# Graph layers on one core: the first two gathers of each layer moved into the block ahead of it

## The chip, the cores and the metric

The kernel runs on 1 core of one Trainium2 chip, in one launch. The metric is the device time of an execution in microseconds (us); the number compared is the median of several runs. A profile is one execution of its own, with its own time.

## What is computed

A graph with 50000 nodes of 64 features and 100000 directed edges (25000 drawn ones in both directions and 50000 self loops, sorted by target) goes through two NGCF layers, then a residual sum and a layer norm:

```python
def _ngcf_conv(x, W1, W2, src, dst, n_nodes):
    deg_out = clip(segment_sum(ones, src), 1.0)
    deg_in = clip(segment_sum(ones, dst), 1.0)
    norm = rsqrt(deg_out[src] * deg_in[dst])
    msg = (x[src] @ W1 + x[src] * x[dst] @ W2) * norm[:, None]
    agg = segment_sum(msg, dst)
    return x @ W1 + agg
h = relu(_ngcf_conv(x, W1_1, W2_1, ...))
h = _ngcf_conv(h, W1_2, W2_2, ...)
out = layernorm(x + h)
```

## The kernel before, in words

Nodes lie in 392 tiles of 128; tile t, lane p is row p * 392 + t of a table in HBM. The program is a chain of blocks, and in a block each engine has its own list of instructions, with waits on semaphores between them.

- **prepare** (the block of lines 84 to 437) reads the edge lists, sorts the edges into 398 chunks of 128 edges of neighbouring targets, counts degrees, makes the norms, and writes `k.row_i` (L422), the table row of each edge's source, and `table0`: x beside its norm, 65 floats a row. The table goes out in six stores on SP's queue (L183), each as soon as its norms are made (L417). SP waits at L184 to L186 until all stores have landed. `spread` (two tiles, written at L392, read by the matmuls at L268) is a work tile of this block alone. GpSimd's last work here is iota at about 22 us; after it the engine has nothing to do in this block.
- **layer** (called twice, its block opens at L516 and following) goes in 51 batches of 8 chunks (the last two have 4 and 2). GpSimd (L652 to L657) issues one indirect DMA a chunk, which gathers 128 rows of the table into `rows`, a ring of 4 batches. Before batch b from the fifth on it waits until batch b - 4 is used up: in layer 0 by VectorE's first step on it (`rows_scaled`, L892), in layer 1 by TensorE's sums (`summed`, L676). Within the list there is no other order. VectorE makes the selection matrices (`select`, L885), in layer 0 also cuts the rows into three bf16 parts (`cut`, L892, L895, L898); TensorE adds up each tile with three matmuls a pair of chunk and tile (`add_up`, L676); then come the node's own row, norms, the product with the weights (L705, L762, L698), relu or layer norm, and the stores: in layer 0 into `table1`, 96 floats a row (L632), in layer 1 into the output (L635). SP waits at L648 until the stores have landed.

Between two blocks stands a barrier over all five engines that the library writes at a block's end. In the compiled program it reads so: TensorE, VectorE, ScalarE and SP each drain, add one to a first semaphore and wait for a second; GpSimd drains, waits until the first has four, and then releases the others with the second. So GpSimd leads: nobody enters the next block before its drain is through. `rows` and the semaphores `gathered` belong to the layer (L527, L559), so no gather can be issued before this barrier.

The only waits between the landing of the last store and the first gather are that barrier's. The same holds ahead of layer 1.

Of the kernel before, what the change touches and what calls it, by code (L numbers as in the profile page):

```python
# [7 lines left out]
P = 128  # L8
N_NODES, D, N_EDGES = 50000, 64, 100000
EPS = 1e-5  # L10
F32 = mybir.dt.float32
I32 = mybir.dt.int32
F16 = mybir.dt.float16
BF16 = mybir.dt.bfloat16
ALU = mybir.AluOpType
# [3 lines left out]
TILES = 392  # L19
# [11 lines left out]
LOW = 1024  # L31


def band(c):

    return range(max(0, (P * c - REACH) // CAP + 1), min(TILES - 1, (P * c + P - 1) // CAP) + 1)
# [18 lines left out]
FRAME_TILE = [4 * p for p in FRAME_P0]  # L55
FRAME_SHIFT = [round((FRAME_TILE[k] + FRAME_TILE[k + 1]) / 2 * (CAP - P) / P) for k in range(FRAMES)]
SPAN = 64
PIECES = [(k, b, 4) for k in range(7) for b in (0, 4)] + [(7, 0, 8), (8, 0, 8)]
LAST_PIECE = [max(i for i, p in enumerate(PIECES) if p[0] == k) for k in range(FRAMES)]

# [19 lines left out]
def prepare(nc, x, src, dst, tables, keepers):  # L80
# [3 lines left out]
    with ExitStack() as ctx:  # L84
        def sb(name, shape, dt=F32):
            return ctx.enter_context(nc.sbuf_tensor("a_" + name, shape, dt))

        def sem(name):
            return ctx.enter_context(nc.semaphore("a_" + name))
# [5 lines left out]
        def scratch(width=RUN, dt=F32):  # L95
# [17 lines left out]
        value_t = [sb(f"value_t{a}", [P, RAWS], F16) for a in range(4)]  # L113
        hot = [sb(f"hot{j}", [P, P, 4 * FRAME_PS[0]], F16) for j in range(3)]
        near_s, near_n = sb("near_s", [P, WIN, EB * FRAME_PS[0]], F16), sb("near_n", [P, WIN, EB * FRAME_PS[0]], F16)
        spread = [sb(f"spread{j}", [P, 4, WIN, EB * FRAME_PS[0]], F16) for j in range(2)]
        node_grid = sb("node_grid", [P, TILES + SPAN])
        root, square = sb("root", [P, TILES]), sb("square", [P, TILES])
        row_f = sb("row_f", [P, CHUNKS])
# [9 lines left out]
        hots_made, spread_made, piece_placed, added = sem("hots_made"), sem("spread_made"), sem("piece_placed"), sem("added")  # L129
        number16_made, differed, deg_made, root_made, norm_step, norm_made = (sem(n) for n in (  # L130
            "number16_made", "differed", "deg_made", "root_made", "norm_step", "norm_made"))
        tail_made, table_out = sem("tail_made"), sem("table_out")
        x_in = [sem(f"x_in{i}") for i in range(len(X_LOADS) + 1)]
        block = ctx.enter_context(nc.Block())

# [52 lines left out]
        @block.gpsimd  # L188
        def _(pool):
            G = nc.gpsimd  # L190
            free = dict(allow_small_or_imprecise_dtypes=True)


            G.iota(num, pattern=[[1, RUN]], base=0, channel_multiplier=RUN, **free).then_inc(built, 1)
            pool.wait_ge(built, 1)
            G.affine_select(out=num, in_=num, compare_op=ALU.is_ge, fill=float(NO_EDGE), base=N_EDGES - 1,
                            pattern=[[-1, RUN]], channel_multiplier=-RUN).then_inc(num_made, 1)
            G.memset(k.ident[:, :], 0.0).then_inc(built, 1)
            pool.wait_ge(built, 2)
            G.affine_select(out=k.ident[:, :], in_=k.ident[:, :], compare_op=ALU.not_equal, fill=1.0,  # L200
                            base=0, pattern=[[-1, P]], channel_multiplier=1).then_inc(built, 1)
            G.memset(step16[:, :], 0.0).then_inc(built, 1)
            G.memset(wrap16[:, :], 0.0).then_inc(built, 1)
            pool.wait_ge(built, 3)
            G.tensor_copy(ident16[:, :], k.ident[:, :]).then_inc(consts, 1)
            G.iota(lanes[:, :, :], pattern=[[1, P], [0, FRAME_PS[0]]], base=0, channel_multiplier=0, **free).then_inc(consts, 1)
            pool.wait_ge(dst_in, 48)
            G.tensor_scalar(shifted_i, d_i[:, 0:RUN], float(-SHIFT * P), None, ALU.add).then_inc(shifted_made, 1)
            G.iota(home[:, :], pattern=[[1, EB // 2], [0, 2], [4, EP]], base=0, channel_multiplier=0, **free).then_inc(consts, 1)
            pool.wait_ge(kept_made, 1)  # L210
            pool.wait_ge(float_made, 1)
            G.tensor_tensor(number, kb, node_f, ALU.subtract).then_inc(built, 1)
            pool.wait_ge(built, 6)
            G.tensor_scalar(number_h, number, float(LOW), 1.0 / 64, ALU.add, ALU.mult).then_inc(number_made, 1)
            G.iota(win_s[:, :, :], pattern=[[1, WIN + max(FRAME_SHIFT)], [0, FRAME_PS[0]]], base=-BACK, channel_multiplier=0, **free).then_inc(consts, 1)
            G.iota(win_n[:, :, :], pattern=[[1, WIN], [0, FRAME_PS[0]]], base=-BACK - SHIFT, channel_multiplier=0, **free).then_inc(consts, 1)
            G.affine_select(out=step16[:, :], in_=step16[:, :], compare_op=ALU.not_equal, fill=64.0,
                            base=0, pattern=[[-1, P]], channel_multiplier=1).then_inc(built, 1)
            pool.wait_ge(built, 7)
            G.affine_select(out=step16[:, :], in_=step16[:, :], compare_op=ALU.not_equal, fill=-64.0,  # L220
                            base=1, pattern=[[-1, P]], channel_multiplier=1).then_inc(consts, 1)
            G.affine_select(out=wrap16[:, :], in_=wrap16[:, :], compare_op=ALU.not_equal, fill=-64.0,
                            base=1 - P, pattern=[[P, P]], channel_multiplier=1).then_inc(consts, 1)
            for i in range(0, LOW + 4 * P, LOW):
                n = min(LOW, LOW + 4 * P - i)
                last = G.iota(k.place[:, i:i + n], pattern=[[1, n]], base=1, channel_multiplier=0, **free)
            last.then_inc(consts, 1)

        @block.tensor
        def _(pe):  # L230
# [92 lines left out]
        def _(dve):  # L323
# [95 lines left out]
            def row_numbers(a, b):  # L419
                step(V.scalar_tensor_tensor(row_f[:, a:b], k.grid[:, 1, BACK + a:BACK + b], float(TILES), k.grid[:, 0, BACK + a:BACK + b], ALU.mult, ALU.add))  # L420
                step(V.tensor_scalar(row_f[:, a:b], row_f[:, a:b], float(-TILES), 0.0, ALU.add, ALU.max))
                V.tensor_single_scalar(k.row_i[:, a:b], row_f[:, a:b], float(P * TILES), op=ALU.min)  # L422


            V.tensor_reduce(k.extreme[0:EP, 1:2], step_up, AX.X, ALU.min).then_inc(checked, 1)
# [47 lines left out]
GROUP = [(t, t + 8) for t in range(0, TILES - 8, 8)] + [(TILES - 8, TILES - 4), (TILES - 4, TILES)]  # L473
GROUPS = len(GROUP)
GN = 8
RING = 4
BANKS = 3

COUNT_AT = [{b: b for b in range(0, 44, 2)}, {b: b for b in range(1, 45, 2)}]
# [33 lines left out]
def layer(nc, l, x, out, tables, flag, keepers):  # L513

    k = keepers
    with ExitStack() as ctx:  # L516
        def sb(name, shape, dt=F32):
            return ctx.enter_context(nc.sbuf_tensor(f"c{l}_" + name, shape, dt))

        def sem(name):  # L520
            return ctx.enter_context(nc.semaphore(f"c{l}_" + name))
# [1 line left out]
        def ps(name, shape):  # L523
            return ctx.enter_context(nc.psum_tensor(f"c{l}_" + name, shape, F32))

        row = (ROW, THREE)[l]
        rows = sb("rows", [P, RING, 8, row])  # L527
        sel = sb("sel", [P, 2, 8, 4 * P], BF16)
        hot_l, hot_t = sb("hot_l", [P, 8, P], F16), sb("hot_t", [P, 8, TILES], F16)
        own = sb("own", [P, 2, GN, D])  # L530
# [8 lines left out]
        else:  # L539
# [16 lines left out]
        tail_out = sem("tail_out")  # L556
        own_end_made, end_in, end_total, settled, w_made, last_made = (sem(n) for n in (
            "own_end_made", "end_in", "end_total", "settled", "w_made", "last_made"))
        gathered = [sem(f"gathered{j}") for j in range(RING)]  # L559
        stored, res_in = [sem(f"stored{j}") for j in range(4)], [sem(f"res_in{j}") for j in range(3)]  # L560
        block = ctx.enter_context(nc.Block())
        x_full = x[0:FULL_TILES * P, :].rearrange("(t p) d -> p t d", p=P)
# [87 lines left out]
        @block.gpsimd  # L650
        def _(pool):
            for b in range(BATCHES):  # L652
                done(pool, (rows_scaled, summed)[l], b - RING + 1)
                for i in range(BATCH[b]):
                    c = FIRST[b] + i
                    nc.gpsimd.indirect_dma_start(out=rows[:, b % RING, i], out_offset=None, in_=tables[l],  # L656
                                                 in_offset=bass.IndirectOffsetOnAxis(ap=k.row_i[:, c:c + 1], axis=0)).then_inc(gathered[b % RING], 16)  # L657

        @block.tensor
        def _(pe):  # L660
# [766 lines left out]
class Kept:  # L1427


    def __init__(k, keep, ctx, weights):  # L1430
        k.weights = weights
        k.ident, k.ones, k.eps = (keep(n, [P, w], F32, ctx) for n, w in (("ident", P), ("ones", 1), ("eps", 1)))
        k.place = keep("place", [P, LOW + 4 * P], F16, ctx)
        k.wcat = keep("wcat", [2 * D, 2, D], F32, ctx)

        k.grid = keep("grid", [P, 3, CHUNKS + 10], F32, ctx)
        k.row_i = keep("row_i", [P, CHUNKS], I32, ctx)

        k.number16 = keep("number16", [P, TILES + 1], F16, ctx)
        k.deg = keep("deg", [P, TILES], F32, ctx)  # L1440
        k.extreme, k.tally = keep("extreme", [P, 2], F32, ctx), keep("tally", [P, 4], F32, ctx)
        k.xh = keep("xh", [P, TILES, ROW], F32, ctx)

# [4 lines left out]
def build(nc, x, src, dst, weights, out, dram):  # L1448
    tables = [dram["table0"], dram["table1"]]
    with ExitStack() as last:  # L1450
        def keep(name, shape, dt=F32, stack=last):
            return stack.enter_context(nc.sbuf_tensor("k_" + name, shape, dt))
        flag = keep("flag", [1, 1], I32)
        with ExitStack() as ctx:
            k = Kept(keep, ctx, weights)
            prepare(nc, x, src, dst, tables, k)
            k.p_count = ctx.enter_context(nc.psum_tensor("k_p_count", [P, 512], F32))
            for l in range(2):
                layer(nc, l, x, out, tables, flag, k)

        def if_needed(eng):
            return eng.If(eng.value_load(flag[0:1, 0:1]) > 0)
        general_path(nc, x, src, dst, weights, out, dram, if_needed)
# [18 lines left out]
```

## Time and profile before

| what | value |
|---|---|
| three runs | 1763.13, 1771.59, 1775.89 us, median 1771.59 |
| profiled execution, its own time | 1784.15 us |
| its span, first to last instruction | 1782.5 us |
| mean granted TensorE clock in it | 0.725 of full speed |

The span is 1.65 us short of the execution's own time, and that is 12.6 us (0.7%) above the median of the three runs, which themselves lie within 0.7%. Times in the rows are microseconds from the span's start. A row's last part in brackets is the idle time of the engine just before it and what ended it; SPq, PEq and POOLq are the queues (sequencers) of these engines.

### The profile page before, as it was taken

The numbers are of one execution on the slowest core, as the hardware profiler recorded it, in microseconds if no ns is written. First come the engines' busy times: TensorE is split into PE (matmuls) and PEld (weight loads), VectorE is DVE, ScalarE is ACT, GpSimd is POOL, SyncE is SP. The second block draws the span as 40 slices with busy tenths as digits, with TensorE's granted clock in tenths as the row PEclk, the third lists the DMA queues.
The fourth block names the chain that finished last, engine by engine and source line by source line (L and its number), as shares of the span: only waits on it lengthen the run. The fifth ranks groups of instructions, "written<-read, shape, count | busy, mean of one in ns | idle before, by whom it ended". The sixth has DMA issues, their size and how long they took to land. (4 is left out here: it accounts for less than half of the span.)

```text
span 1782.5 us, 33246 instructions
## 1 busy us (share of the span) xinstructions
PE 998.9 (56%) x12938; PEld 862.4 (48%) x12938; DVE 1001.7 (56%) x2595; ACT 741.0 (42%) x2743; POOL 789.1 (44%) x819
## 2 busy tenths in 40 slices
PE   2641455565456456644665526666666666666666
PEld 2530344454355345544555525555555555555556
DVE  9982354555355445543565714665656656656556
ACT  2000144454354434543455602444444445444445
POOL 4007454344434443454343165555554555545540
PEclk9999866676676666766667856767767777767767
DMA  7951011111111111111111211222322222222222
GB/s 146 244 214 27 15 37 35 31 42 44 37 31 43 44 34 31 42 45 35 31 43 41 88 35 36 59 62 63 78 63 62 63 63 63 63 62 63 63 62 51
DMA packets 148569, 106.57 MB, mean 60 GB/s; under 512 B 115832, under 2 KB 128568, under 8 KB 147900
## 3 DMA queue, kind: packets, MB, share of 16 engines
q1 hardware_dynamic: 122728, 71.17, 14.6%
q0 software_dynamic: 25472, 32.86, 10.0%
q8 instruction: 102, 1.67, 0.4%
q10 hardware_dynamic: 212, 0.42, 0.1%
q14 instruction: 55, 0.45, 0.1%
HBM read 59.27 MB, written 45.11 MB: 59 GB/s over the span
## 5 line engine op out<-in xcount | busy, mean ns | idle before, releaser
L656 POOL DMA_INDIRECT c_rows<-table,k_row_i x796 | 768.2, 965 | 952.5 <-DVE c_yr L892 342.3
L676 PE MATMUL c_sum<-c_rows,c_sel 128*128 128x64 bf16 x4665 | 267.6, 224 | 274.6 <-issue 253.8
L762 ACT ACTIVATE c_uvt<-c_turn 128x512 f32<-128x512 f32 x196 | 106.6, 595 | 705.6 <-PE c_turn L705 703.0
L676 PEld LDWEIGHTS c_sum<-c_rows,c_sel 128*128 128x128 bf16 x4665 | 233.3, 119 | 307.6 <-issue 304.2
L930 DVE TENSOR_TENSOR c_sum<-c_sum,c_own 128x512 f32<-128x512 f32 x94 | 65.6, 698 | 507.5 <-PE c_sum L676 495.2
L676 PE MATMUL c_sum<-c_rest,c_sel 128*128 128x64 bf16 x1555 | 223.0, 219 | 134.3 <-issue 134.3
L676 PE MATMUL c_sum<-c_yr,c_sel 128*128 128x64 bf16 x1555 | 223.4, 219 | 131.3 <-issue 106.8
L676 PE MATMUL c_sum<-c_lo,c_sel 128*128 128x64 bf16 x1555 | 223.8, 219 | 109.4 <-issue 109.2
L885 DVE TENSOR_SCALAR c_sel<-k_place,k_grid 128x512 bf16<-128x512 f16 (+2 forms) x796 | 228.9, 358 | 86.0 <-PE c_sum L676 86.0
L676 PEld LDWEIGHTS c_sum<-c_yr,c_sel 128*128 128x128 bf16 x1555 | 177.3, 117 | 155.8 <-issue 155.6
L676 PEld LDWEIGHTS c_sum<-c_rest,c_sel 128*128 128x128 bf16 x1555 | 173.9, 115 | 143.4 <-issue 143.0
L698 PE MATMUL c_out<-k_wcat,c_uvt 128*128 128x64 f32 x1504 | 206.0, 295 | 59.9 <-ACT c_uvt L762 46.0
L698 PEld LDWEIGHTS c_out<-k_wcat,c_uvt 128*128 128x128 f32 x1504 | 193.6, 208 | 87.1 <-ACT c_uvt L762 65.9
L676 PEld LDWEIGHTS c_sum<-c_lo,c_sel 128*128 128x128 bf16 x1555 | 173.9, 115 | 120.0 <-issue 119.6
L754 ACT ACTIVATE c_sum<-c_sum,k_xh 128x64 f32<-128x64 f32 x752 | 161.6, 317 | 156.9 <-DVE c_sum L930 156.9
L741 ACT ACTIVATE c_own<-k_xh 128x64 f32<-128x64 f32 x752 | 193.4, 398 | 9.9 <-PEq L84 7.7
L705 PE MATMUL c_turn<-k_ident,c_uv 128*128 128x128 f32 x784 | 147.1, 350 | 0.7 <-DVE c_uv L968 0.7
L918 DVE TENSOR_SCALAR c_hot_t<-k_place,k_grid 128x392 f16<-128x392 f16 x398 | 131.6, 331 | 0.0
L705 PEld LDWEIGHTS c_turn<-k_ident,c_uv 128*128 128x128 f32 x784 | 122.5, 187 | 1.0 <-DVE c_uv L968 1.0
L967 DVE TENSOR_TENSOR c_uv<-c_sum,k_xh 128x512 f32<-128x512 f32 (+1 forms) x100 | 67.7, 677 | 85.9 <-ACT c_sum L754 49.3
L917 DVE TENSOR_SCALAR c_hot_l<-k_place,k_grid 128x128 f16<-128x128 f16 x398 | 99.0, 249 | 0.0
L807 ACT ACTIVATE c_y<-c_z,c_rstd 128x64 f32<-128x64 f32 x368 | 93.7, 371 | 0.3 <-DVE c_rstd L1010 0.3
(162 smaller groups left out, 1053.2 us busy)
## 6 DMA issues: line engine op xcount, KB each, us to landing
table<-c_y SPq DMA_DIRECT2D x48, 384.0 KB
c_rows<-table,k_row_i POOLq DMA_INDIRECT x796
out<-c_y SPq DMA_DIRECT2D x48, 256.0 KB
c_res<-in_x SPq DMA_DIRECT2D x46, 256.0 KB
table<-k_xh SPq DMA_DIRECT2D x2, 3640.0 KB, 10.9
table<-k_xh SPq DMA_DIRECT2D x1, 3542.5 KB, 12.1
table<-k_xh SPq DMA_DIRECT2D x1, 1040.0 KB, 7.0
c_res_end<-in_x SPq DMA_DIRECT2D x1, 704.0 KB, 6.3
```

The costliest lines, as they stand in the source:

```text
L656: nc.gpsimd.indirect_dma_start(out=rows[:, b % RING, i], out_offset=None, in_=tables[l], in_offset=bass.IndirectOffsetOnAxis(ap=k.row_i[:, ...
L676: last = nc.tensor.matmul(p_sum[g % BANKS][:, t - GROUP[g][0], :], sel[:, b % 2, i, n * P:(n + 1) * P], part[:, i], start=first and q == 0 ...
L698: last = nc.tensor.matmul(out_bank(g)[:, n, :], uvt[:, g % 2, n, :], weights, start=True, stop=True)
L705: last = nc.tensor.transpose(turn_bank(g, n)[:, n % 4, :], uv[:, g % 2, n].rearrange("p a d -> p (a d)"), k.ident[:, :])
L741: last = A(own[:, g % 2, t - a, :], k.xh[:, t, 0:D], ACT.Copy, scale=k.xh[:, t, D:ROW])
L754: last = A(p_sum[g % BANKS][:, t - a, :], p_sum[g % BANKS][:, t - a, :], ACT.Copy, scale=k.xh[:, t, D:ROW])
L762: last = A(uvt[:, g % 2, h:h + 4, :], turn_bank(g, h)[:, :, :], ACT.Copy)
L807: last = A(y[:, g % 4, n, :], z[:, g % 4, n, :], ACT.Copy, scale=rstd[:, g % 4, n:n + 1])
L885: last = V.tensor_scalar(sel[:, b % 2, i, 0:w], k.place[:, a:a + w], k.grid[:, 2, BACK + c:BACK + c + 1], None, ALU.is_equal)
L917: V.tensor_scalar(hot_l[:, m], k.place[:, 0:P], k.grid[:, 1, slot], None, ALU.is_equal)
L918: last = V.tensor_scalar(hot_t[:, m], k.place[:, 0:TILES], k.grid[:, 0, slot], None, ALU.is_equal)
L967: V.tensor_tensor(uv[:, j, 0:w, 0, :], bank[:, 0:w], h, ALU.add)
```

## The change

`rows` becomes a part of a tile `k.ring` that is kept over all blocks, and so do the semaphores `gathered`. In prepare the two `spread` tiles lie in the same memory. GpSimd's list in prepare gets three waits at its end (row numbers made, the zero rows and the six stores landed) and then chunks 0 and 1 of layer 0's batch 0. Its list in layer 0 gets four waits at its end (all stores of `table1` landed) and then chunks 0 and 1 of layer 1. Both layers start at chunk 2.

```diff
+RING = 4
+BEGUN = 2
+def ring_of(k, l):
+    row = (ROW, THREE)[l]
+    return k.ring[:, 0:RING * 8 * row].rearrange("p (r c d) -> p r c d", r=RING, c=8)
+
+def gather(nc, k, l, tables, b, i):
+    c = FIRST[b] + i
+    return nc.gpsimd.indirect_dma_start(out=ring_of(k, l)[:, b % RING, i], out_offset=None, in_=tables[l],
+                                        in_offset=bass.IndirectOffsetOnAxis(ap=k.row_i[:, c:c + 1], axis=0)).then_inc(k.gathered[l][b % RING], 16)
...
+SPREAD = 4 * WIN * EB * FRAME_PS[0]
...
-        spread = [sb(f"spread{j}", [P, 4, WIN, EB * FRAME_PS[0]], F16) for j in range(2)]
+        spread = [k.ring[:, j * SPREAD // 2:(j + 1) * SPREAD // 2].bitcast(F16).rearrange("p (a w r) -> p a w r", a=4, w=WIN) for j in range(2)]
...
@@ prepare, gpsimd, at the end
             last.then_inc(consts, 1)
+            pool.wait_ge(rows_made, 2)
+            pool.wait_ge(zero_out, 32)
+            pool.wait_ge(table_out, 16 * len(NORM_TILES))
+            for i in range(BEGUN):
+                gather(nc, k, 0, tables, 0, i)
...
@@ prepare, vector, row_numbers
-                V.tensor_single_scalar(k.row_i[:, a:b], row_f[:, a:b], float(P * TILES), op=ALU.min)
+                V.tensor_single_scalar(k.row_i[:, a:b], row_f[:, a:b], float(P * TILES), op=ALU.min).then_inc(rows_made, 1)
...
@@ layer
-        row = (ROW, THREE)[l]
-        rows = sb("rows", [P, RING, 8, row])
+        rows, gathered = ring_of(k, l), k.gathered[l]
...
-        gathered = [sem(f"gathered{j}") for j in range(RING)]
...
@@ layer, gpsimd
                 done(pool, (rows_scaled, summed)[l], b - RING + 1)
-                for i in range(BATCH[b]):
-                    c = FIRST[b] + i
-                    nc.gpsimd.indirect_dma_start(out=rows[:, b % RING, i], out_offset=None, in_=tables[l],
-                                                 in_offset=bass.IndirectOffsetOnAxis(ap=k.row_i[:, c:c + 1], axis=0)).then_inc(gathered[b % RING], 16)
+                for i in range(BEGUN if b == 0 else 0, BATCH[b]):
+                    gather(nc, k, l, tables, b, i)
+            if l == 0:
+                for j in range(4):
+                    pool.wait_ge(stored[j], 16 * len(range(j, GROUPS, 4)))
+                for i in range(BEGUN):
+                    gather(nc, k, 1, tables, 0, i)
...
@@ Kept
+        k.ring = keep("ring", [P, max(RING * 8 * THREE, 2 * SPREAD // 2)], F32, ctx)
+        k.gathered = [[ctx.enter_context(nc.semaphore(f"k_gathered{l}_{j}")) for j in range(RING)] for l in range(2)]
```

## Rows read from the trace of the kernel before

**Rows 1.** The page, part 1: busy us, share of the span, instructions

```profile
PE 998.9 (56%) x12938; PEld 862.4 (48%) x12938; DVE 1001.7 (56%) x2595; ACT 741.0 (42%) x2743; POOL 789.1 (44%) x819
```

**Rows 2.** The page, part 5: groups; busy, mean ns | idle before, releaser

```profile
L656 POOL DMA_INDIRECT c_rows<-table,k_row_i x796 | 768.2, 965 | 952.5 <-DVE c_yr L892 342.3
L676 PE MATMUL c_sum<-c_rows,c_sel 128*128 128x64 bf16 x4665 | 267.6, 224 | 274.6 <-issue 253.8
...
L676 PE MATMUL c_sum<-c_rest,c_sel 128*128 128x64 bf16 x1555 | 223.0, 219 | 134.3 <-issue 134.3
```

**Rows 3.** Timeline of layer 0's first 20 us: start, us, engine, line

```profile
123.36 0.67 SPq L183 DMA_DIRECT2D table<-k_xh  x1
129.34 2.02 ACT L741 ACTIVATE c_own<-k_xh 128x64 f32<-128x64 f32 x8 [7.73 <-PEq L84]
129.37 0.15 DVE L1014 TENSOR_SCALAR c_checks<-k_extreme 128x1 f32<-128x1 f32 x1 [6.04 <-PEq L84]
130.10 1.17 POOL L656 DMA_INDIRECT c_rows<-table,k_row_i  x1 [107.78 <-POOLq L84]
...
131.58 0.94 POOL L656 DMA_INDIRECT c_rows<-table,k_row_i  x1 [0.30 <-issue]
132.83 0.94 POOL L656 DMA_INDIRECT c_rows<-table,k_row_i  x1 [0.30 <-issue]
```

**Rows 4.** Waits of SP's queue: us in total, times, longest us

```profile
SPq L186 <- DMA table<-k_xh: 4.8, 1, 4.8
...
SPq L648 <- DMA table<-c_y: 1.5, 1, 1.5
```

**Rows 5.** Timeline where layer 1 begins

```profile
1011.36 2.30 SPq L632 DMA_DIRECT2D table<-c_y  x3
...
1015.69 2.02 ACT L741 ACTIVATE c_own<-k_xh 128x64 f32<-128x64 f32 x8 [2.15 <-PEq L516]
...
1016.31 0.99 POOL L656 DMA_INDIRECT c_rows<-table,k_row_i  x1 [41.73 <-POOLq L516]
1017.60 0.94 POOL L656 DMA_INDIRECT c_rows<-table,k_row_i  x1 [0.30 <-issue]
1018.84 0.94 POOL L656 DMA_INDIRECT c_rows<-table,k_row_i  x1 [0.30 <-issue]
```

**Rows 6.** Chain of waits from layer 1's start: start, us, what

```profile
1015.55 0.02 POOLq L516
1015.56 0.74 issue
1016.31 0.99 POOL c_rows L656
...
1025.08 2.24 DMA c_rows<-table,k_row_i
...
1027.69 2.50 PE c_sum L676 x44
...
1045.53 2.59 issue
1048.11 0.21 PE c_sum L676
```

**Rows 7.** Timeline of a wait for VectorE's cut in mid layer 0

```profile
751.94 1.27 POOL L656 DMA_INDIRECT c_rows<-table,k_row_i  x1 [16.26 <-DVE c_yr L892]
...
751.00 0.68 DVE L892 TENSOR_TENSOR c_yr<-c_rows 128x512 f32<-128x512 f32 x1
```

**Rows 8.** Timeline of VectorE at both layers' starts

```profile
131.55 2.34 DVE L885 TENSOR_SCALAR c_sel<-k_place,k_grid 128x128 bf16<-128x128 f16 x8
141.61 0.69 DVE L892 TENSOR_TENSOR c_yr<-c_rows 128x512 f32<-128x512 f32 x1 [7.72 <-DMA c_rows<-table,k_row_i]
...
198.18 1.93 DVE L885 TENSOR_SCALAR c_sel<-k_place,k_grid 128x512 bf16<-128x512 f16 x7 [44.21 <-PE c_sum L676]
...
1015.93 4.49 DVE L885 TENSOR_SCALAR c_sel<-k_place,k_grid 128x128 bf16<-128x128 f16 x16
1062.25 2.54 DVE L885 TENSOR_SCALAR c_sel<-k_place,k_grid 128x512 bf16<-128x512 f16 x8 [41.83 <-PE c_sum L676]
```

**Rows 9.** Busy us by stretch; PE, PEld, DVE, ACT, POOL, clock, DMA share, GB/s

```profile
130.00:190.00 60.00, 6.25 (x60) 4.16 (x61) 13.72 (x43) 1.36 (x6) 45.57 (x48) 1.00 0.17 27
190.00:200.00 10.00, 3.86 (x22) 1.99 (x22) 1.82 (x7) 0.00 (x0) 0.25 (x1) 1.00 0.03 4
1016.00:1056.00 40.00, 5.55 (x60) 3.91 (x60) 4.42 (x17) 1.71 (x8) 30.24 (x32) 0.50 0.28 58
```

More of the change, by code:

```diff
@@ L131, in prepare @@
             "number16_made", "differed", "deg_made", "root_made", "norm_step", "norm_made"))
-        tail_made, table_out = sem("tail_made"), sem("table_out")
+        tail_made, table_out, rows_made = sem("tail_made"), sem("table_out"), sem("rows_made")
         x_in = [sem(f"x_in{i}") for i in range(len(X_LOADS) + 1)]
@@ L475 @@
 GN = 8
-RING = 4
 BANKS = 3
@@ L1427, with __init__ @@
 class Kept:
-    def __init__(k, keep, ctx, weights):
+    def __init__(k, nc, keep, ctx, weights):
         k.weights = weights
@@ L1454, in build @@
         with ExitStack() as ctx:
-            k = Kept(keep, ctx, weights)
+            k = Kept(nc, keep, ctx, weights)
             prepare(nc, x, src, dst, tables, k)
```

## The prediction

> **What bounds the kernel now.** I read the page first. No engine is busy for much over half of the span [rows 1], so the time is made of waits. The widest groups say which: GpSimd idles for 952.5 us before its gathers, mostly for VectorE's cuts, and TensorE's sums idle for 274.6 us on "issue", time in which nothing that the profile shows was awaited [rows 2]. So in the middle of a layer GpSimd has slack, and a gather is worth nothing there. It can be worth something only where the ring is empty, at the two starts, so I went to the timeline and the chain of waits there.
>
> Layer 0's start: the last table store is issued at 123.36 and SP's queue is through with it at 124.03 [rows 3]; SP then waits 4.8 us for its landing [rows 4], so it lands at about 128.83. ScalarE and VectorE begin in the new block at 129.34 and 129.37, GpSimd's first gather at 130.10 [rows 3]: 1.27 us after the landing. Layer 1's start: the last store leaves SP's queue at 1011.36 + 2.30 = 1013.66 [rows 5], SP waits 1.5 us [rows 4], landing at 1015.16. GpSimd releases the barrier at 1015.55 [rows 6], ScalarE begins at 1015.69, the first gather at 1016.31 [rows 5]: 1.15 us after the landing. Both starts lie on the path that sets the end: VectorE waits 7.72 us for layer 0's first batch [rows 8], and the chain of waits goes through layer 1's first eight gathers and the landing of the eighth to TensorE's first sum at 1027.69 [rows 6].
>
> What follows the first sum matters too. TensorE does some 50 of batch 0's 75 matmuls at full pace and then creeps, with pauses of up to 2.59 us for one matmul of 0.21 us [rows 6]: 60 matmuls in 60 us in layer 0 and 60 in 40 us in layer 1, while GpSimd issues 48 and 32 gathers one behind the other [rows 9]. Batch 0's sum is done at 198.18 and 1062.25, where VectorE's select goes on [rows 8], some 8 and 6 us after GpSimd's run of gathers has ended. I take it that the creep ends when GpSimd's run does, so that what GpSimd gains at a start is gained one for one.
>
> **The change part by part.** First the gathers. A gather occupies GpSimd for 0.94 us, the next starts 0.30 us later, and a first one takes up to 1.17 us [rows 3] or 1.27 us [rows 7]. Two of them, from the first's start to the third's, are 132.83 - 130.10 = 2.73 us in layer 0 [rows 3] and 1018.84 - 1016.31 = 2.53 us in layer 1 [rows 5]. Were both wholly hidden, 5.3 us would be gained: that is the most. But nothing new hides them. They can't start before the table has landed, and that is the very event that opens the barrier. All there is to overlap is the barrier's own passage, 1.27 and 1.15 us. And GpSimd leads that barrier: its drain stands behind the two gathers, so the release waits for them, and the other four engines are held.
>
> Layer 0, step by step. From a wait that opens to a gather's start, GpSimd needs 751.94 - (751.00 + 0.68) = 0.26 us [rows 7]. So the first gather starts at 128.83 + 0.26 = 129.09. The second follows as before after 131.58 - 130.10 = 1.48 us, at 130.57, and ends at 131.51. Then drain, barrier, branch. From GpSimd's release to its first gather it was 0.76 us (0.02 and 0.74) in layer 1 [rows 6]. The drain and the check of the four signals, all there by then, no row shows. They cost no less than nothing and no more than the 0.39 us from landing to release in layer 1 (1015.16 to 1015.55), in which SP's own drain lies too; I take 0.1, since SP's steps fall away. The third gather thus starts at 131.51 + 0.1 + 0.76 = 132.37, before at 132.83: 0.46 us gained, between 0.17 and 0.56.
>
> Layer 1: first gather at 1015.16 + 0.26 = 1015.42, the second 1.29 us later at 1016.71, its end at 1017.65, third at 1018.51, before at 1018.84: 0.33 us gained, between 0.04 and 0.43. The four waits on `stored` stand behind a GpSimd that idled for 41.73 us [rows 5], and three of the four are open long before; they cost nothing.
>
> Second, the others are released later. ScalarE begins 0.14 us after the release in layer 1 [rows 5, 6], so the release was at about 129.2 in layer 0; now it is at 131.6, and in layer 1 at 1017.75 instead of 1015.55: later by 2.4 and 2.2 us. Queued behind are ScalarE's own rows, VectorE's checks and selects and SP's fetches. VectorE's select ends at 133.89 and the engine then waits till 141.61 [rows 8]: 7.7 us of cover for 2.4. In layer 1 its 16 selects end at 1020.42, and TensorE wants them only with the rows at 1027.69. So this costs nothing; without the cover it would be 4.6 us in all. Third, the signal on the row numbers and GpSimd's waits in prepare: the engine was idle for 107.78 us [rows 3]; nothing stands behind them but the barrier. Fourth, the ring's new place. `spread` is last read before the stores land, so no wait comes from sharing. The same matmul reading two tiles in different places takes 219 and 224 ns on the mean [rows 2], so place costs nothing that I can see.
>
> Sum: -0.46 - 0.33 = -0.8 us. The profiled execution goes from 1784.15 to 1783.3, and against the median of the runs, 12.6 us lower, that is 1771.6 - 0.8 = 1770.8.
>
> Whether the drain holds the release at all is what no row shows. [...]
>
> **The rivals.** (1) GpSimd's drain does not wait for gathers that are still being worked off: the release comes at once and the third gather follows the second after 0.30 us. Third gathers at 129.09 + 1.48 + 1.25 = 131.82 and 1015.42 + 1.29 + 1.25 = 1017.96: gains of 1.01 and 0.88, 1769.7 in all. For it: GpSimd's own queue and its engine are separate rows in the trace. Against: a drain that waits for nothing would be none.
>
> (2) Slower: the drain waits until the two gathers have landed. From its start to its landing a gather takes 2.24 us [rows 6], of which 0.94 is the engine's, so each barrier opens 1.3 us later: -0.8 + 2.6 = +1.8, 1773.4. It turns slower as soon as the drain takes over 0.56 us in layer 0 and 0.43 in layer 1. Against: nobody in the kernel waits for a landing without its semaphore. [...]
>
> (3) TensorE's creep is not tied to GpSimd's run as I take it: a start that falls otherwise costs batch 0 one more pause, 2.59 + 0.21 = 2.8 us in each layer [rows 6], +5.6 - 0.8 = +4.8, 1776.4, or spares one, -6.4, 1765.2. For it: the pauses come in sizes, not evenly. Against: GpSimd's runs of 48 and 32 gathers stay as long, and TensorE's list is untouched.
>
> (4) The change doesn't do what it says: the two gathers don't start before the release, for instance since the last store is seen later by GpSimd than by SP. Then it is 0, 1771.6.
>
> **How the numbers follow.** The forecast gets 0.6, rival 1 0.12, rival 2 0.1, rival 3 0.1 (half each way), rival 4 0.05, and 0.03 is left for an effect of the new places in memory that I don't see. All named cases lie between -6.4 and +4.8 us, within 0.4% of the time. About 1% (18 us) is what a measurement of this kernel can tell from no change, and the three runs alone spread over 12.8 us. So the range is made by the runs' spread: the median shown lies 8.5 above the lowest and 4.3 below the highest run, and with the cases that gives 1761 to 1780. Within 1%: 0.95; faster by over 1%: 0.02; slower: 0.03.
>
> **What would show it.** In the changed profile GpSimd should have two gathers that start about 0.3 us after the landing, and ScalarE's and VectorE's first instructions of the block some 2.3 us later than before against that landing. The distance from the second gather's start to the third's should be about 1.8 us instead of 1.25; 1.25 speaks for rival 1, over 3 for rival 2. Landing to third gather should be 3.5 us (before 4.0) in layer 0 and 3.35 (before 3.7) in layer 1. VectorE's first cut should start 0.4 us nearer to the landing, and select's first wait for a sum in each layer should end earlier by as much. A total that moves by over 10 us, or a sum of batch 0 that ends more than 3 us off these, would prove me wrong about what bounds the start.

## The result, and the profile after

Over 22 runs of each, the changed kernel takes 1775.29 us and the kernel before 1767.72: a ratio of 1.0041, 95% interval 1.0027 to 1.0056. It is slower by 7.6 us, between 5 and 10. The forecast was 0.8 us faster. (The three runs shown before had their median at 1771.59.) In every ratio here a run that lies over 1.5% above the fastest of its kernel is left out, as one of E3's was; the medians keep it.

The two profiled executions say the opposite at first sight: the span is now 1772.8 us and was 1782.5. A single execution scatters by more than the effect: the profiled one of the kernel before, 1784.15 us, lay above all 22 of its timed runs, whose highest was 1775.89. So only stretches that begin and end at the same events are compared here.

First the timeline where layer 0 begins, one engine after the other (GpSimd, ScalarE, VectorE); L47 is the line of the gathers now, and the row of SP's queue is the last two table stores:

```profile
122.36 1.63 SPq L202 DMA_DIRECT2D table<-k_xh  x2
...
129.66 1.17 POOL L47 DMA_INDIRECT k_ring<-table,k_row_i  x1 [107.34 <-DMA table<-k_xh]
131.13 0.94 POOL L47 DMA_INDIRECT k_ring<-table,k_row_i  x1 [0.30 <-issue]
134.63 1.03 POOL L47 DMA_INDIRECT k_ring<-table,k_row_i  x1 [2.56 <-POOLq L103]
...
134.00 2.02 ACT L765 ACTIVATE c_own<-k_xh 128x64 f32<-128x64 f32 x8 [12.45 <-PEq L103]
...
143.55 0.76 DVE L916 TENSOR_TENSOR c_yr<-k_ring 128x512 f32<-128x512 f32 x1 [5.14 <-DMA k_ring<-table,k_row_i]
...
199.70 2.19 DVE L909 TENSOR_SCALAR c_sel<-k_place,k_grid 128x512 bf16<-128x512 f16 x8 [43.72 <-PE c_sum L700]
```

The same where layer 1 begins, from the timelines of SP's queue, GpSimd, ScalarE, TensorE and VectorE:

```profile
986.40 15.84 SPq L653 DMA_DIRECT2D table<-c_y  x6
...
1004.52 0.94 POOL L47 DMA_INDIRECT k_ring<-table,k_row_i  x1 [40.71 <-DMA table<-c_y]
1005.77 0.94 POOL L47 DMA_INDIRECT k_ring<-table,k_row_i  x1 [0.31 <-issue]
1016.83 0.98 POOL L47 DMA_INDIRECT k_ring<-table,k_row_i  x1 [10.11 <-POOLq L539]
...
1016.20 2.02 ACT L765 ACTIVATE c_own<-k_xh 128x64 f32<-128x64 f32 x8 [14.09 <-PEq L539]
...
1025.71 2.59 PE L700 MATMUL c_sum<-k_ring,c_sel 128*128 128x64 bf16 x45 [25.52 <-DMA k_ring<-table,k_row_i]
...
1059.38 2.54 DVE L909 TENSOR_SCALAR c_sel<-k_place,k_grid 128x512 bf16<-128x512 f16 x8 [38.45 <-PE c_sum L700]
```

And the waits of SP's queue (us in total, times, longest), of which the kernel before had only the two on DMA at these lengths [rows 4]:

```profile
SPq L539 <- PEq L539: 12.3, 2, 12.1
...
SPq L103 <- PEq L103: 4.9, 1, 4.9
SPq L205 <- DMA table<-k_xh: 4.8, 1, 4.8
...
SPq L669 <- DMA table<-c_y: 1.5, 1, 1.5
```

The reader is to see three things. The two gathers do start ahead of the barrier. Behind the second one, GpSimd's next start is released by its own queue 2.56 and 10.11 us later, where it was 0.30 us [rows 3, 5]. And every other engine stands in the barrier meanwhile: SP for 4.9 and 12.1 us after its stores have landed. Measured from the landing (as in the prediction: end of SP's queue row plus SP's wait, 123.99 + 4.8 = 128.79 and 1002.24 + 1.5 = 1003.74):

| from the last store's landing to | layer 0 before | layer 0 after | layer 1 before | layer 1 after |
|---|---|---|---|---|
| first gather starts | 1.27 | 0.87 | 1.15 | 0.78 |
| third gather starts | 4.00 | 5.84 | 3.68 | 13.09 |
| VectorE's select behind batch 0's sum | 69.35 | 70.91 | 47.09 | 55.64 |

The trace also records the barrier's own instructions, each engine's drain and the steps on the two semaphores, which the views leave out. Their starts, in us (of GpSimd's drain both ends):

| | layer 0 before | layer 0 after | layer 1 before | layer 1 after |
|---|---|---|---|---|
| drains of TensorE, ScalarE, VectorE | 120.93, 121.40, 123.17 | 120.88, 121.35, 123.11 | 1008.79, 1011.85, 1011.86 | 997.38, 1001.15, 1001.15 |
| SP's drain | 129.09 | 129.02 | 1015.43 | 1004.02 |
| GpSimd's drain | 19.63 to 22.40 | 129.88 to 133.76 | 971.82 to 983.62 | 1004.76 to 1015.92 |
| GpSimd passes the first semaphore | 129.12 | 133.79 | 1015.46 | 1015.97 |
| GpSimd raises the second | 129.21 | 133.87 | 1015.55 | 1016.06 |
| the four others pass it | 129.25 to 129.26 | 133.91 to 133.92 | 1015.59 to 1015.60 | 1016.10 to 1016.11 |

In the kernel before SP's drain is the last of the five, in the changed one GpSimd's, and the other four pass within 0.06 us of GpSimd's release in all four cases. The record of GpSimd's drain begins while gathers ahead of it still run (in layer 1 after, 1.95 us before the second one's end).

So layer 0's start is 1.6 to 1.8 us later and layer 1's 8.6 to 9.4. The sum of the last line's two differences, 10.1 us, lies just above the upper end of what the timing says.

### The profile page after: what moved, and what is told of

The parts are those of the page before. It is cut to its first block and busy times, and to the rows that moved or that the text cites. A ratio compares the mean times of both kernels' runs of the same rounds, so it can differ in the third digit from the quotient of the medians.

```text
span 1772.8 us, 33249 instructions
## 1 busy us (share of the span) xinstructions
PE 994.5 (56%) x12938; PEld 854.3 (48%) x12938; DVE 1000.1 (56%) x2595; ACT 739.9 (42%) x2743; POOL 789.0 (45%) x819
## 3 DMA queue, kind: packets, MB, share of 16 engines
q0 software_dynamic: 25472, 32.86, 10.1%
## 5 line engine op out<-in xcount | busy, mean ns | idle before, releaser
L47 POOL DMA_INDIRECT k_ring<-table,k_row_i x796 | 768.1, 965 | 942.6 <-DVE c_yr L916 329.5
L700 PE MATMUL c_sum<-k_ring,c_sel 128*128 128x64 bf16 x4665 | 267.2, 225 | 268.3 <-issue 239.3
L700 PEld LDWEIGHTS c_sum<-k_ring,c_sel 128*128 128x128 bf16 x4665 | 233.9, 120 | 300.4 <-issue 296.6
L700 PE MATMUL c_sum<-c_rest,c_sel 128*128 128x64 bf16 x1555 | 212.6, 213 | 135.0 <-issue 135.0
L700 PE MATMUL c_sum<-c_yr,c_sel 128*128 128x64 bf16 x1555 | 213.9, 214 | 120.0 <-issue 94.4
L700 PE MATMUL c_sum<-c_lo,c_sel 128*128 128x64 bf16 x1555 | 214.2, 214 | 111.4 <-issue 111.4
L700 PEld LDWEIGHTS c_sum<-c_lo,c_sel 128*128 128x128 bf16 x1555 | 166.3, 111 | 146.2 <-issue 145.5
L700 PEld LDWEIGHTS c_sum<-c_yr,c_sel 128*128 128x128 bf16 x1555 | 169.9, 113 | 137.5 <-issue 136.8
L700 PEld LDWEIGHTS c_sum<-c_rest,c_sel 128*128 128x128 bf16 x1555 | 166.6, 111 | 129.0 <-issue 128.7
```

The source lines that it names most:

```text
L47: return nc.gpsimd.indirect_dma_start(out=ring_of(k, l)[:, b % RING, i], out_offset=None, in_=tables[l], in_offset=bass.IndirectOffsetOnAx ...
L700: last = nc.tensor.matmul(p_sum[g % BANKS][:, t - GROUP[g][0], :], sel[:, b % 2, i, n * P:(n + 1) * P], part[:, i], start=first and q == 0 ...
```

## The experiments

The question was what keeps GpSimd's queue for 10 us in one barrier and 2.5 in the other. Theory A: GpSimd's drain, which stands behind the two gathers. By the theory it waits for their landing and then works off something for the gathers issued since its last drain, of which there are 2 in the first case and 398 in the second (396 in layer 0 and the 2 moved). In the kernel before the same drain ended at 983.62, while the engine idled for 41.73 us [rows 5]. The rivals are in the expectations.

The experiments ran on three other chips (one for each letter), where the kernel before takes some 1198 us instead of 1768; the time of each is compared with runs of the kernel before on the same chip. These chips don't show TensorE's creep. The stretches of the run that changes only the ring's place (F1 below) say so; the columns are those of [rows 9], where TensorE did 60 matmuls in each of the first and third stretch:

```profile
130.00:190.00 60.00, 30.76 (x524) 28.70 (x524) 39.19 (x112) 17.90 (x70) 45.89 (x47) 0.86 0.17 27
...
664.00:704.00 40.00, 19.56 (x324) 18.29 (x325) 17.43 (x60) 8.24 (x34) 30.25 (x33) 0.67 0.24 50
```

Here GpSimd's gathers are the bound: within a layer they follow each other without a pause, 242.1 us of its 371.3 idle us being the 0.30 us between two of them (F1's page, part 5):

```profile
L47 POOL DMA_INDIRECT k_ring<-table,k_row_i x796 | 772.6, 971 | 371.3 <-issue 242.1
```

That makes these chips the better place for this question: a late third gather delays all that follow. The two gaps themselves are the same as on the first chip, within 0.02 us (F2). In the edits "..." marks what is left out.

**E1 and E2, one start alone.**

```diff
E1, layer 0 alone:
-                for i in range(BEGUN if b == 0 else 0, BATCH[b]):
+                for i in range(BEGUN if b == 0 and l == 0 else 0, BATCH[b]):
...
-            if l == 0:
-                for j in range(4):
-                    pool.wait_ge(stored[j], ...)
-                for i in range(BEGUN):
-                    gather(nc, k, 1, tables, 0, i)
E2, layer 1 alone:
-            pool.wait_ge(rows_made, 2)
-            pool.wait_ge(zero_out, 32)
-            pool.wait_ge(table_out, 16 * len(NORM_TILES))
-            for i in range(BEGUN):
-                gather(nc, k, 0, tables, 0, i)
...
-                for i in range(BEGUN if b == 0 else 0, BATCH[b]):
+                for i in range(BEGUN if b == 0 and l == 1 else 0, BATCH[b]):
```

> Only the two gathers ahead of layer 0 are moved; layer 1 starts as before. Theory A (backlog): GpSimd's drain in the barrier waits for the landing of its gathers and then works off something for every gather issued since the last drain. With 2 gathers behind it, the gap from the second gather's end to the third's start is 2.6 us as in the changed kernel, landing to third gather 5.8 us (before 4.0), and layer 1's first gather follows the landing by 1.15 us as before. Total: +1.8 us against before, 0.1%, which the timing can hardly tell from nothing. Theory B (the drain is long for any gather still in flight): the same here. Theory C (the time comes from the ring's new place in memory): the total is about +7 us, since the ring is moved here too.

> Only the two gathers ahead of layer 1 are moved. Theories A and B: the gap between the second and third gather of layer 1 is about 10.1 us, landing to third gather 12.6 us (before 3.7), batch 0's sum 8 us later against the landing; total +8 us, ratio 1.0045. Theory C (place in memory): total about +7 us as in the run with layer 0 alone, with no tie to this gap.

E1: 1203.73 against 1198.46 us, ratio 1.0044 (1.0028 to 1.0060). E2: 1205.82, ratio 1.0059 (1.0024 to 1.0093). GpSimd's timelines, E1's at layer 0 and E2's at layer 1:

```profile
134.66 1.03 POOL L47 DMA_INDIRECT k_ring<-table,k_row_i  x1 [2.58 <-POOLq L103]
```

```profile
663.70 0.94 POOL L47 DMA_INDIRECT k_ring<-table,k_row_i  x1 [22.38 <-DMA table<-c_y]
...
676.00 0.99 POOL L47 DMA_INDIRECT k_ring<-table,k_row_i  x1 [10.11 <-POOLq L534]
```

Each gap comes with its own two gathers and is independent of the other. E2's total is the one expected. E1's is 5.3 us above before where 1.8 were expected, and its interval excludes 1.8. Its rows show nothing at the start beyond the 1.8; F1 asks whether the rest is the ring's place.

**E3, a drain set where the engine idles.** The changed kernel with

```diff
             if l == 0:
+                pool.drain()
                 for j in range(4):
                     pool.wait_ge(stored[j], ...)
```

> The changed kernel with one more GpSimd drain in layer 0, behind its last own gather and ahead of the waits for the table's stores, where the engine idles some 40 us. Theory A (backlog of all gathers since the last drain): the barrier's own drain has only two gathers behind it, the gap ahead of layer 1's third gather falls from 10.1 to about 2.6 us, landing to third gather 5.1 us; total about +3 us against before instead of +7.6. Theory B (any gather in flight makes the drain long, whatever was drained before): the gap stays 10 us and the total +7.6.

```profile
668.54 0.94 POOL L47 DMA_INDIRECT k_ring<-table,k_row_i  x1 [26.57 <-DMA table<-c_y]
...
673.25 0.98 POOL L47 DMA_INDIRECT k_ring<-table,k_row_i  x1 [2.52 <-POOLq L539]
```

The gap ahead of layer 1's third gather falls from 10.11 to 2.52 us (the barrier's drain is over at 672.35), as theory A said and theory B, by which any gather in flight makes the drain long, did not. The total is weaker evidence: the ratio 1.0025 (1.0002 to 1.0048) is the 3 us expected, but the medians, 1204.86 and 1198.46, are 6.4 us apart. With two gathers behind the last drain the gap is 2.5 us; the other 7.6 are for what was issued before them.

**E4 and F3, no drain of GpSimd.** The changed kernel with

```diff
-        block = ctx.enter_context(nc.Block())
+        block = ctx.enter_context(nc.Block(no_gpsimd_drain=True))
...
-                last = G.iota(k.place[:, i:i + n], ...)
-            last.then_inc(consts, 1)
+                last = G.iota(k.place[:, i:i + n], ...).then_inc(consts, 1)
+            pool.wait_ge(consts, 9)
```

in E4 for prepare and the layers, in F3 also for the block of the fallback at the program's end.

> The changed kernel with blocks that end in a barrier by semaphores alone: GpSimd doesn't drain (the place array's iotas get their own semaphore wait in its stead). Theories A and B: both gaps go; the third gather starts within 0.3 to 1.2 us of the second's end, landing to third gather 3.0 to 3.9 us at both starts; total between -2 and 0 us against before, so the whole 7.6 us of the change come from the drain. Theory C (place in memory): the gaps go but the total stays several us above before.

> The changed kernel with no GpSimd drain at the end of any block, the last one (the fallback's, at the program's end) included. In the run that left the drain only there, SP waited 8.9 us for it at the very end. Theory A: that wait falls to under 1 us, and the total is 1 to 2 us below before (the gain of 0.98 and 0.88 us that the two starts should show). Theory D (without drains the gathers of layer 1 themselves get slower): no wait at the end, but the time between layer 1's third and last gather is still some us longer than with drains.

E4's total was a miss: 1206.70 us, ratio 1.0066 (1.0038 to 1.0095), although both gaps were gone. SP's waits told where it went; E4's, then F3's:

```profile
SPq L1171 <- PEq L1171: 8.9, 1, 8.9
```

```profile
SPq L539 <- PEq L539: 1.0, 2, 0.8
...
SPq L1171 <- PEq L1171: 0.4, 1, 0.4
```

L1171 is the fallback's block, which does nothing here but still drained: all 796 gathers were undrained, and the price came at the program's end, where nothing hides it. E4's trace has that drain of GpSimd from 1195.75 to 1204.81, while the drains of the other four begin by 1196.28. It also tells waiting from working off. E4's last gather in GpSimd's timeline is

```profile
1164.79 0.94 POOL L47 DMA_INDIRECT k_ring<-table,k_row_i  x1 [0.30 <-issue]
```

and SP's 8.9 us lie near the end of a span of 1205.0 us, behind the last work on the output at 1192. The last signal of a gather's landing is at 1168.28. So no gather had been in flight for 27 us when the drain began, and the wait was 8.5 us longer than F3's 0.4 all the same: this is no wait for a gather's landing.

Without that drain too (F3) the time is 1198.04 against 1198.98 us, ratio 0.9990 (0.9959 to 1.0020), and 0.9% below the changed kernel on the same chip (F2). GpSimd's timelines of F3 at layer 0's and layer 1's start:

```profile
131.14 0.95 POOL L47 DMA_INDIRECT k_ring<-table,k_row_i  x1 [0.30 <-issue]
132.40 0.98 POOL L47 DMA_INDIRECT k_ring<-table,k_row_i  x1 [0.30 <-issue]
```

```profile
661.58 0.94 POOL L47 DMA_INDIRECT k_ring<-table,k_row_i  x1 [21.85 <-DMA table<-c_y]
...
665.48 0.99 POOL L47 DMA_INDIRECT k_ring<-table,k_row_i  x1 [0.46 <-issue]
```

The third gather follows the second after the usual 0.30 us at both starts. The gather at 665.48 is the fourth, and its 0.46 us of idle time is the only one there above 0.31. Theory D, by which layer 1's gathers get slower without drains, is refuted: from the third to the last of them it is 501.7 us in F3 and 501.4 in F2. So once the drain is gone the change costs nothing that these runs can tell; whether it then gains its fraction of a us can't be told either.

**F1, F2 and G3, the controls.** F1 is the changed kernel with all gathers back behind the barriers, F2 the changed kernel itself, G3 the kernel before without any drain of GpSimd (the edits of F3).

> The changed kernel with no gather moved: the ring is kept over all blocks and shares its memory with spread, and that is all. Theory A (GpSimd's drain is the whole cost): the same time as before, within 0.2%, and both first gathers about 1.2 us behind the landing. Theory C (part of the cost is the place in memory): 3 to 4 us above before, which is what the run with layer 0 alone had beyond its 1.8 us.

> The changed kernel itself on the chip of these experiments, where the kernel before takes some 1198 us and GpSimd's gathers run without a pause. Theory A: third gathers later against the landing by 1.8 and 8.9 us, and here nothing between can take it up, so +9 to +10.5 us, ratio about 1.008.

> The kernel before without any GpSimd drain at a block's end. Before, layer 0's own drain lies in the 21 us (here) or 41 us in which the engine waits for the last store, so it costs nothing and taking it away brings nothing: within 0.2% of before, landing to first gather about 1.2 us. Were the drain also on the path in the kernel before, it would be faster by some 8 us, 0.7%.

F1: 1198.42 us, ratio 0.9995 (0.9969 to 1.0020). The place in memory costs nothing that this chip can tell, so E1's extra 3.5 us (on another chip) are hardly from there; they stay unexplained. F2: 1209.27 us, ratio 1.0084 (1.0051 to 1.0117), +10.3 us, within the range expected, with the same two gaps:

```profile
134.65 1.02 POOL L47 DMA_INDIRECT k_ring<-table,k_row_i  x1 [2.54 <-POOLq L103]
...
675.76 0.98 POOL L47 DMA_INDIRECT k_ring<-table,k_row_i  x1 [10.11 <-POOLq L539]
```

G3: 1199.73 us, ratio 1.0003 (0.9979 to 1.0026), which excludes the 8 us that a drain on the path would have given. In the kernel before the drain was hidden, as the 41.73 us of idle time had it: it was over at 983.62, 31.8 us before SP's began.

**F4, G1 and G2, the price of a drain.** F4 and G1 put drains among the gathers of the kernel before, in the middle of a batch (F4's edit; G1 has batches 11 and 35 in layer 0, 19 and 48 in layer 1):

```diff
                 for i in range(BATCH[b]):
+                    if i == 4 and b in (2, 3, 7, 15, 31, 47):
+                        pool.drain()
```

G2 is the changed kernel with BEGUN = 1.

> The kernel before with GpSimd drains set among the gathers of both layers, in the middle of batches 2, 3, 7, 15, 31 and 47, so that 20, 8, 32, 64, 128 and 128 gathers have been issued since the last drain. Theory A (a price for each gather since the last drain): the gap before the next gather is about 2.5 us for the short ones and grows with the count by some 0.02 us a gather, to about 5 us for 128. Theory B (the price is that of the position or of any gather in flight): all gaps of a layer are alike. Theory E (the price is of what was issued since the program's start): gaps grow through layer 0 and layer 1's are above all of layer 0's.

> The kernel before with two more GpSimd drains in each layer, in the middle of batches 11 and 35 of layer 0 and 19 and 48 of layer 1, so that 92, 192, 156 and 232 gathers have been issued since the last drain. The run with six drains a layer gave 2.7, 3.3, 3.5 to 4.4 and 6.0 us for 8, 20, 32 and 64 gathers and 3.7 to 4.5 us for 128. Theory A as first stated (a price for each gather since the last drain, 0.06 us by those four) gives 7.6, 13.7, 11.5 and 16 us. Theory A2 (it grows only up to some number of gathers, where the gathers themselves clear it, and starts anew) gives gaps that are all between 2.5 and about 10 us and don't rise in the order of the counts.

> The changed kernel with one gather moved at each start instead of two. If the drain's price is of what lies behind it in the layer, the gap from the moved gather's end to the next gather's start is again about 10 us ahead of layer 1 and 2.5 us ahead of layer 0. If it is a price for each moved gather, it is half, 5 us and 1.3 to 2 us.

GpSimd's timeline of F4, the gathers behind the drains of layer 0 (20, 8, 32, 64, 128 and 128 gathers since the last drain):

```profile
159.22 0.94 POOL L658 DMA_INDIRECT c_rows<-table,k_row_i  x1 [3.33 <-issue]
...
171.69 0.94 POOL L658 DMA_INDIRECT c_rows<-table,k_row_i  x1 [2.70 <-issue]
...
215.90 1.01 POOL L658 DMA_INDIRECT c_rows<-table,k_row_i  x1 [3.53 <-issue]
...
304.04 1.13 POOL L658 DMA_INDIRECT c_rows<-table,k_row_i  x1 [5.99 <-issue]
...
471.14 1.19 POOL L658 DMA_INDIRECT c_rows<-table,k_row_i  x1 [3.70 <-issue]
...
639.71 0.94 POOL L658 DMA_INDIRECT c_rows<-table,k_row_i  x1 [4.52 <-issue]
```

and G1's (92, 192, 156 and 232):

```profile
257.05 0.94 POOL L658 DMA_INDIRECT c_rows<-table,k_row_i  x1 [8.29 <-issue]
...
512.57 0.94 POOL L658 DMA_INDIRECT c_rows<-table,k_row_i  x1 [8.94 <-issue]
...
882.74 0.94 POOL L658 DMA_INDIRECT c_rows<-table,k_row_i  x1 [5.66 <-issue]
...
1181.54 0.94 POOL L658 DMA_INDIRECT c_rows<-table,k_row_i  x1 [4.35 <-issue]
```

In order of the count: 8 gathers 2.7 us, 20: 3.3, 32: 3.5 (4.4 in layer 1), 64: 6.0, 92: 8.3, 128: 3.7 and 4.5, 156: 5.7, 192: 8.9, 232: 4.4, and 398 in the changed kernel 10.1. The other five gaps in F4's layer 1 are within 0.3 us of layer 0's. F4 and G1 were run once each, at 1247.67 and 1225.88 us; their gaps, less 0.30 us each, add up to 44.6 and 26.0 us, beside 48.7 and 27.2 above the kernel before. So the totals bear the gaps out.

The price rises by 0.07 us a gather on the mean from 8 to 92, and falls back at least twice on the way to 398. A price for each gather since the last drain, as theory A first had it, is refuted by the 128, 156 and 232; so is theory E, a price of all gathers since the program's start, as layer 1's gaps aren't above layer 0's. What is left is A2, a price between 2.5 and some 10 us that grows with the count but comes down from time to time by itself. What brings it down was not tried. An estimate fitted afterwards to these same rows, and put to no run: 1.7 us, plus 0.08 us for each gather that is left over when the count is divided by 101, comes within 0.8 us of every gap measured, and of E4's 8.9 us for 796.

In G2 the gaps behind the one moved gather are

```profile
133.33 1.03 POOL L47 DMA_INDIRECT k_ring<-table,k_row_i  x1 [2.49 <-POOLq L103]
```

```profile
675.13 0.98 POOL L47 DMA_INDIRECT k_ring<-table,k_row_i  x1 [10.03 <-POOLq L539]
```

so one gather moved gives the same gaps as two (2.56 and 10.11 us): one ahead of the barrier puts the whole drain on the path here. G2's one run took 1208.36 us, beside 1198.68 for the kernel before.

**G4, a pause after two batches.**

```diff
                 done(pool, (rows_scaled, summed)[l], b - RING + 1)
+                if b == 2:
+                    pool.wait_ge(summed, 1)
```

> The kernel before, but in each layer GpSimd waits ahead of batch 2 until TensorE has summed batch 0. The prediction took it that TensorE's creep through batch 0 ends when GpSimd's first run of gathers does. If so, and if this chip shows the creep, batch 0's sum ends within some 5 us of its start instead of 50, and the total falls. If this chip shows no creep (the kernel before takes 1198 us), batch 0's sum ends within 5 us anyway and GpSimd loses only the wait, a few us a layer.

1197.38 us in one run, beside 1198.68 for the kernel before. This chip shows no creep (521 matmuls between 130 and 190 us in this run), and the gathers of layer 0 around batch 2 still follow each other after 0.30 us, so the wait was open when GpSimd came to it. The run says nothing of the creep. Whether the creep on the first chip ends with GpSimd's run stays open.

## Why the prediction was wrong

**What bounds the start: right.** Both starts lie on the path. In the changed kernel's trace the third gather's delay, 1.84 and 9.41 us, reaches batch 0's sum at 1.56 and 8.55. The prediction had named a batch 0's sum over 3 us off as the sign that it was wrong here; layer 1's is 8.9 us off (55.64 against 47.09 - 0.33), but the delay came with the gathers, so the sign points at the price of the barrier and not at what bounds the start.

**GpSimd leads the barrier, and the gathers stand before its drain: right.** This was read from the program, and the trace has it: GpSimd raises the second semaphore at 133.87 and 1016.06, 0.11 and 0.14 us after its own drain, while the other four had stood in the barrier since 129.02 and 1004.02. Rival 1, the release that comes at once, is refuted: the gaps are 2.56 and 10.11 us. That the drain holds the release for the gathers was my assumption; no row of the kernel before showed it. It fits these runs but falls short of them. In layer 0 the last signal of the second gather's landing is at 133.62 and the release at 133.87, 0.25 us later. In layer 1 the landing is at 1008.22 and the release 7.8 us later, and E4's 8.9 us came with no gather in flight. I had given the drain 0.1 us, and its price decided. That the 2.5 us of a nearly empty drain are a wait for the landing, and not a fixed price, no run here separates.

**The step that failed: the drain's price.** "They cost no less than nothing and no more than the 0.39 us from landing to release in layer 1 ... I take 0.1." Of the measured gaps I had 0.1 + 0.76 = 0.86 us; they are 1.7 and 9.25 us longer. The bound was taken from the wrong engine. The 0.39 us held SP's drain (1015.43) and GpSimd's release (1015.55), but GpSimd's own drain had run from 971.82 to 983.62, in its idle time, 9.04 us of it behind the last gather's end (1016.31 - 41.73 = 974.58). None of my rows shows it, and the upper end was no bound. The wide idle time of 41.73 us was in my rows; I read it as free room for the new waits, while it was also the cover of the drain that the change moves out of it.

**Rival 2 was nearest, but lacked what layer 1's barrier cost.** It said that the drain waits for the landing, 1.3 us at each start. For layer 0 that is close: 1.3 expected, 1.7 measured beyond my 0.86. E3 and G2 show the same 2.5 us gap wherever few gathers have been issued since the last drain. For layer 1 it lacked the backlog: 7.6 us of the 10.1 go when a drain is set earlier (E3). By rival 2 the total was +1.8 us, measured +7.6.

**From a wait that opens to the first gather: 0.26 us, measured 0.87 and 0.78.** I took it from a gather that waits for VectorE [rows 7]. A gather that waits for a DMA's landing starts 0.5 to 0.6 us later. With it even the best case shrinks: without any drain (F3) the third gather starts 3.62 us after the landing in layer 0, against 4.00 before, a gain of 0.4 us and not of the 1.0 that rival 1 had.

**The others' cover: enough, but thinner than forecast.** They were held 5.2 us after the landing (ScalarE at 134.00) instead of the 2.9 forecast (131.74 - 128.83); VectorE still had 5.14 us to wait for its rows. In layer 1 they were held till 1016.20, 12.5 us after the landing. That cost nothing of its own, since the third gather, at 1016.83, was as late as they.

**The ring's place and the waits in prepare: nothing, as forecast** (F1 for the place; F3, which has the waits too, for both). **The range** held the measured 1775.3, but by the scatter of the runs, and not by the right term: the cases reached up to +4.8 us, and +7.6 is outside of them. Its upper end follows from its terms (1770.8 + 4.3 + 4.8 = 1780); its lower end by the same sum would be 1770.8 - 8.5 - 6.4 = 1756, not 1761. That it stays within 1% was right.

## What to carry to other kernels

In this kernel a barrier was not only a wait for the slowest engine: each of the five drained in it, and GpSimd's drain, which cost nothing behind 41.73 us of idle time, held layer 1's release for 7.8 us beyond their landing once two gathers stood in front of it. Before moving a step across a barrier, ask which engine leads it, what its drain may have to wait for, and where in the trace that drain lies; here it ran under cover, 11.80 us long, and nothing on the path gave a bound of its price. If gathers must be in flight across the barrier, drop GpSimd's drain there and give each thing that it ordered a semaphore, at the program's last block too. In this kernel that took the cost away (F3: ratio 0.9990; E4, which kept the last block's drain, had 1.0066), and brought no gain over the kernel before that the runs could tell.

## What the runs showed that I had not expected

In these runs a drain of GpSimd behind indirect gathers left a gap of some 2.5 us when few had been issued since the last one, 8.3 us at 92 gathers, and between 3.7 and 10.1 us at 128 to 400, without rising steadily with the count. In E4 the drains that were left out were paid at the next one: 8.9 us at the program's end for 796 gathers, 27 us after the last had landed.

The same kernel takes 1768 us on one chip and 1198 us on the others. The granted TensorE clock was 0.725 of full speed in the one profile and 0.838 in F1's, but what stands out is TensorE's creep while GpSimd gathers: 60 matmuls in 60 us against 524. How much of the difference it makes, its cause and its end were not found here.
